# Moving the transposes of the next unit, and their copy out of PSUM, to the head of each step of a projection loop

## The reference, cut to what matters

```
zn = layer_norm(z)                       # over the 64 channels
a  = mask * sigmoid(zn @ w_ag + b_ag) * (zn @ w_ap + b_ap)
b  = mask * sigmoid(zn @ w_bg + b_bg) * (zn @ w_bp + b_bp)
g  = sigmoid(zn @ w_g + b_g)
p  = einsum('bikc,bjkc->bijc', a, b)
x  = z_in + (layer_norm(p) @ w_z + b_z) * g
```

## Time and profile before

| | |
|---|---|
| median of 3 runs | 1984.49 us (1982.11 to 1986.62) |
| the profiled execution | 1978.67 us, of which its span is 1976.8 us |
| PE busy in the span | 1604.1 us (81%) |
| ACT busy in the span | 1168.0 us (59%) |
| DVE busy in the span | 1445.7 us (73%) |
| POOL busy in the span | 1039.7 us (53%) |
| projection stage of layer 0 | from the start to about 284 us |
| projection stage of layer 1 | about 830 to 1164 us |

### The profile page before, as it was taken

The page is one execution under the profiler, slowest core; times in us unless marked ns, Lnnn a source line. Parts: engine busy times, 40 slices in busy tenths (PEclk is TensorE's granted clock), DMA queues, the critical chain, the costliest instruction groups (busy, mean ns, idle before and its releaser), DMA issues. The chain is left out here.

```text
span 1976.8 us, 38230 instructions
## 1 busy us (share of the span) xinstructions
PE 1604.1 (81%) x10716; PEld 1065.7 (54%) x10716; DVE 1445.7 (73%) x4747; ACT 1168.0 (59%) x2726; POOL 1039.7 (53%) x1722
## 2 busy tenths in 40 slices
PE   4778857998758989788888849997747999999997
PEld 2444437786644568644444428786645444444442
DVE  5888850256879979778888840456964999999986
ACT  5898864432217979567777745332227666666651
POOL 4777740145777800066666630245865666666642
PEclk9999988999899989889999979998975999999999
DMA  3686754489886463046776655588966666666652
GB/s 112 176 214 185 208 141 137 146 267 299 266 286 190 129 261 129 21 146 198 220 222 200 192 138 159 168 288 281 285 224 158 184 180 183 185 186 186 181 139 86
DMA packets 387911, 373.40 MB, mean 189 GB/s; under 512 B 155040, under 2 KB 303264, under 8 KB 385696
## 3 DMA queue, kind: packets, MB, share of 16 engines
q1 hardware_dynamic: 342688, 304.32, 52.9%
q10 hardware_dynamic: 45056, 67.13, 10.4%
HBM read 186.80 MB, written 150.99 MB: 171 GB/s over the span
## 5 line engine op out<-in xcount | busy, mean ns | idle before, releaser
L1509 DVE TENSOR_TENSOR ex_xe<-ex_spread,ex_xd 128x512 f32<-128x512 f32 x512 | 317.6, 683 | 20.3 <-PE ex_spread L1760 17.0
L474 ACT ACTIVATE cp_sig<-cp_pv 128x384 f32<-128x384 f32 x512 | 250.5, 494 | 112.1 <-PE cp_pv L525 111.8
L1776 PE MATMUL ex_po<-ex_xe,ex_expert 128*64 128x512 f32 x1024 | 249.1, 607 | 0.0
L525 PE MATMUL cp_pv<-conv_weight,cp_zt 64*128 64x320 f32 x1024 | 189.2, 467 | 52.3 <-ACT cp_zt L465 46.2
L525 PE MATMUL cp_pv<-cp_weight,cp_zt 64*128 64x320 f32 x1024 | 174.7, 458 | 51.7 <-ACT cp_zt L465 44.5
L454 ACT ACTIVATE cp_xn<-cp_x,cp_lift,cp_rstd 128x64 f32<-128x64 f32 x512 | 196.2, 438 | 34.4 <-POOL cp_lift L402 34.4
L1631 ACT ACTIVATE ex_xn<-ex_x,ex_lift,ex_rstd 128x64 f32<-128x64 f32 x512 | 182.0, 429 | 21.0 <-POOL ex_lift L1553 21.0
L429 POOL TENSOR_TENSOR cp_b_stage<-cp_b_stage,cp_mask 128x256 f32<-128x256 f32 x256 | 151.4, 612 | 57.6 <-DVE cp_b_stage L353 57.6
L804 POOL TENSOR_TENSOR cc_p<-cc_p,cc_room 128x512 f32<-128x512 f32 x64 | 106.2, 1659 | 139.8 <-DVE cc_room L775 136.0
L351 DVE SCALAR_TENSOR_TENSOR wx<-cp_pv,cp_mask,cp_sig 128x64 f32<-128x64 f32 x512 | 131.8, 321 | 61.9 <-ACT cp_sig L474 61.7
L1599 POOL TENSOR_TENSOR ex_rest<-ex_turned,ex_rest 128x512 f32<-128x512 f32 x64 | 81.8, 1277 | 172.1 <-ACT ex_turned L1691 172.1
(11 more groups left out here) (209 smaller groups left out, 3655.4 us busy)
## 6 DMA issues: line engine op xcount, KB each, us to landing
gate_scratch<-cp_sig SPq DMA_DIRECT2D x128, 256.0 KB, 2.5
b_scratch<-cp_b_stage SPq DMA_DIRECT2D x128, 256.0 KB, 3.8
cc_room<-b_scratch SPq DMA_DIRECT2D x128, 256.0 KB, 2.7
ex_xd<-ex_xt SPq DMA_DIRECT2D x256, 128.0 KB, 2.5
cp_x<-in_x SPq DMA_DIRECT2D x64, 256.0 KB, 3.2
cc_room<-gate_scratch ACTq DMA_DIRECT2D x64, 256.0 KB, 4.3
cc_p<-in_x SPq DMA_DIRECT2D x64, 256.0 KB, 4.2
after_conv<-cc_p ACTq DMA_DIRECT2D x64, 256.0 KB, 3.8
```

Source lines behind the costliest of these rows:

```text
L474: act.activation(sig[u.mod(2)][:, :, :, i, :].rearrange("p k h c -> p h k c"), pv[slot(u, i)][:, :, 0:3 * C].rearrange("p h (k c) -> p h k ...
L525: pe.matmul(pv[slot(u, i)][:, h, 0:COLS], zt[u.mod(2)][half, i * P:(i + 1) * P], weight[half, :], start=True, stop=True).then_inc(v_made, 1)
L1509: dve.tensor_tensor(xe[u.mod(2)][:, :, h, i * P:(i + 1) * P], pb[k][:].rearrange("p (e t) -> p e t", e=EP), xd[u.mod(8)][:, h, i * P:(i + ...
L1776: ins = pe.matmul(po[h * HALF:(h + 1) * HALF, :], expert[:, e, :], xe[u.mod(2)][:, e, h, :], start=e == 0, stop=e == EP - 1)
```

## The change

In `conv_project`, in the step of ACT, `take(s + 1)` moves from between the third and the fourth row's gates to the head of the step. In the step of PE, `flip(s + 1)` moves from behind row 1 to the head of the step, ahead of all four rows of unit s. `turn_y(s + 8)` moves from between rows 0 and 1 to between rows 1 and 2. No instruction is added or removed, and no wait changes its semaphore or its value.

```diff
@@ -476,11 +476,11 @@
                                    ACT.Sigmoid).then_inc(sig_made, 1)
 
                 def step(s):
+                    take(s + 1)
                     gates(s, 0)
                     gates(s, 1)
                     normalise(s + 2, 0)
                     gates(s, 2)
-                    take(s + 1)
                     gates(s, 3)
                     normalise(s + 2, 1)
 
@@ -526,10 +526,10 @@
                                   start=True, stop=True).then_inc(v_made, 1)
 
                 def step(s):
+                    flip(s + 1)
                     project(s, 0)
+                    project(s, 1)
                     turn_y(s + 8)
-                    project(s, 1)
-                    flip(s + 1)
                     project(s, 2)
                     project(s, 3)
```

## The result

The changed kernel takes 2069.9 us (median of 4 runs, 2065.3 to 2077.0) against 1983.3 before (4 runs): a ratio of 1.045, 95% interval 1.043 to 1.047. It is slower, as predicted, and by 87 us where the sum said 81. The profiled execution has a span of 2063.4 us, 86.6 more than the 1976.8 before.

A forecast was written before the change was run, and what follows sets the result against it. No engine is full; a loop through PE and ACT's copy sets the pace. The change makes an ACT-PE round trip: 57.0 us in layer 0 plus 24.0 in layer 1, +81, so 2064 us, range 2040 to 2112.

The forecast's parts named there:

- the sum: Both layers' longer periods, 57.0 us in layer 0 and 24.0 in layer 1: +81 us on the profiled execution.
- The old loop: Layer 0 before: transposes, row 2, its gates, ACT's copy, row 0, transposes, 4.02 us; opened without new waits, 3.61.
- The transposes wait for ACT's last normalisation: Head of PE's step: PE stands still until ACT's `cp_xn` is ready, some 1.2 us in each step.
- The terms of the new step: Layer 0, built from the transposes through row 3, its gates and ACT's normalisations: period 4.94 us against 4.02, +0.92.
- Row 3's wait for DVE: Layer 0: row 3 needs row 0's PSUM buffer, which DVE must have used up, so starts at 2.81 us.
- Layer 1: Steps with `turn_y`, which sets row 3's start: period 5.32 us against 5.00, +0.32; 24.0 us for the stage.
- The copy hidden behind row 0: Head of ACT's step: the copy ends at 1.27 us, 0.20 before the gates of row 0, and costs nothing.
- The clock: Rival, 8%: PE's clock falls to 1.2 GHz, giving about 2200 us, or near 2370 with layer 1.
- The ends: Stage ends: second transposes some 1.1 us earlier, against a longer first step (1 us) and last step (0.5): together nothing.
- the input is ready: Rival, 3%: the transposes at the head of PE's step never wait, so the kernel gets faster, 1897 us.
- the gaps match: Rival, 2%: PE's new gap replaces the old one exactly, and the kernel stays at 1984 us.
- POOL comes last: Rival, 2%: in every fourth step PE waits for one more POOL operation, 0.62 us, giving 2083 us.

The follow-up runs named there:

- e6: Kernel before, with only ACT's copy one place earlier, ahead of the gates of row 2: 1921.7 us, ratio 0.970.
- e4: Changed kernel with ACT's last two normalisations one place earlier, ahead of the gates of row 3: 1980.7 us, ratio 1.000 to the kernel before.
- e5: Changed kernel with all four normalisations ahead of the gates of row 2: 1934.9 us, ratio 0.977 to the kernel before.
- e7: Changed kernel with three buffers of `cp_xn`, normalisation one unit further ahead, POOL's refinement in one step: 1932.7 us, ratio 0.975 to the kernel before.
- e3: Changed kernel with `turn_y` back between rows 0 and 1: 2096.6 us, ratio 1.057 to the kernel before.
- e2: Changed kernel with ACT's order of before, so only PE's half of the change: 2112.9 us, ratio 1.065 to the kernel before.
- e8: Changed kernel with four more transposes, whose output nothing reads, in PE's pause in layer 0: 2059.0 us, ratio 1.038 to the kernel before.
- e1: Changed kernel with PE's order of before, so only ACT's half of the change: 2114.9 us, ratio 1.068 to the kernel before.

## Why the prediction was right, point by point

- **The old loop and what opening it is worth.** Right, and shown by e6. I named 3.61 as the floor of layer 0; it came to 3.72.
- **The transposes wait for ACT's last normalisation.** Right in place and size: 1.26 us against "some 1.2". e4, e5 and e7 shorten or remove that wait in three ways, and the loss shrinks or goes with it. ACT's wait for the transposes was 0.77, just below the "0.8 to 0.9".
- **The terms of the new step.** The sum for layer 0 was 4.94 and the step is 4.95, partly by luck. Row 0 to its gates took 0.97 (201.17 to 202.14), not the 0.88 of row 2, and so all behind it came 0.08 later. The last step before had shown 0.93 for a row that PE had waited for (280.31 to 281.24). On the other side, row 3 to its gates took 0.85 and not 0.88, and the end of the normalisation to the transposes 0.06 (205.48 to 205.54) and not 0.10. Row 3's wait for DVE, taken from the last step of the stage, was there: 2.89 behind the transposes where I said 2.81.
- **Layer 1.** 5.27 against 5.32: there `turn_y` and not row 0 sets row 3, so only the shorter waits behind ACT count. The stage's sum, 24.0 against 24.3, hit because 3.5 us of single steps made up for the 0.06 us a step.
- **The copy hidden behind row 0.** Right: ACT still waits 0.26 us for row 0 after it, where I had put the cover at 0.20.
- **The clock.** "The granted clock stays at 1.00" was wrong: it was 0.96 over layer 0. The clock was a rival at 8% in a form that did not occur, all of a stage at 1.2 GHz. What occurred is that rival in small: eight steps lengthened by 1.0 to 1.2 us, 8.7 us in sum. It is the term that is missing in the sum. My yardstick, 58% busy at half clock and 72% at full, foresaw neither this nor that e3 has 0.96 at 73%. The section of the Trainium skill that I held against the trace ("TensorE: Matmul & The Clock Gate", "A second HAM failure mode: psum-queue depth-cycling") describes this swing between the two levels. The trace of before did not agree with it; those of the changed kernel and of e2 do, and e8 shows that filling the pause ends it.
- **The ends.** The earlier second transposes were right for layer 0 (-1.2 us). For layer 1 they gave -2.6 instead of some -1.1; I had not looked at its start by itself. The longer first step behind them, put at 1 us, was longer by 0.4 us than the period explains in layer 0 (6.46 against 5.11) and by 2.1 in layer 1 (7.85 against 5.50).
- **The other rivals.** That the input is ready, that the gaps match, and that POOL comes last: none occurred.

## What to carry to other kernels

Before moving an operation to the head of a step, look at what its own input is: if that is the last thing another engine does in the step before, the move turns a slack of a step into a round trip, and everything queued behind it pays. To open a loop, move the one operation that closes it by as few places as needed: the copy one place earlier gained 3.0%, to the head of the step together with its producer it lost 4.5%. And when a loop is opened and nothing moves, look for a second one of the same length before giving up the reading.

## What the runs showed of the hardware that was not expected

- With PE busy 68% of the time and one pause of 1.25 us in each step of 4.95, the granted clock fell to 1.2 GHz eight times between 35 and 340; with the pause at 0.66 us and PE busy 78% (e8) it stayed at 2.4 GHz. In layer 1 the changed kernel has the same pause of 1.28 us, but PE busy 76% of 270 us, and there the clock was 1.00 over 930 to 1200. So the pause alone does not decide. Nor does the busy time: over 930 to 1200 it was 0.96 in e3, with PE busy 73%, and 1.00 in e1, with 72%. What does decide stays open. The most falls are in layer 0 of e2: 0.90, with PE busy 68% and a pause of 1.39 us.
- What a fall costs depends on the loop. In the changed kernel, with PE in the loop, it lengthened one step by 1.0 to 1.2 us. In e1 the clock fell six times between 35 and 340 (0.97), and each fall lengthened two neighbouring steps by 0.4 to 0.5 us, 0.8 to 0.9 together. There PE waits 1.1 us for DVE in each step; whether this wait takes up the rest was not tested.
- In the changed kernel row 0, behind transposes that PE had waited for, has its gates 0.97 us after its start, in both layers; row 2 behind transposes without a wait had them after 0.88. The copy that ACT makes in between is not the reason: in e2, where ACT has none there, it is 0.96 (202.05 to 203.01). What makes the difference was not tested.
